# Cross-attention and FP4 feed-forward on one core: the softmax's turn moved from TensorE to transposing DMAs, in slots of four heads

## The reference, cut to what matters

```python
x = x + xattn(layernorm(x), ctx)       # q from x, k and v from ctx
    logits = einsum('bhqk,bhnk->bhqn', q, k) / 8
    attn   = softmax(logits)           # over the 154 context rows
    heads  = einsum('bhqn,bhnv->bhqv', attn, v);  out = hid @ w_out.T
x = x + ffn(layernorm(x))              # 704 wide
    fp4_linear(x, w): x and w are each rounded to FP4 in blocks of 16, then einsum
    out = fp4_linear(silu(gate) * up, w_down)
```

## Time and profile before

| | |
|---|---|
| runs | 435.9, 433.01 and 435.87 us, median 435.87 |
| profiled execution | span 431.8 us from the first to the last instruction; no time of its own stands beside it |
| PE, DVE, ACT, POOL busy | 367.8, 348.9, 276.8, 200.1 us |
| mean granted clock of TensorE | 0.968 |

### The profile page before, as it was taken

How to read it: one execution, slowest core, us unless ns; L and a number is a source line. 1 busy time by engine, 2 the same in 40 slices (tenths; PEclk the granted TensorE clock), 3 DMA queues, 4 the chain that set the end, 5 groups by cost and what they waited for, 6 DMA issues and landing times.

```text
span 431.8 us, 9502 instructions
## 1 busy us (share of the span) xinstructions
PE 367.8 (85%) x3691; PEld 282.7 (65%) x3691; DVE 348.9 (81%) x676; ACT 276.8 (64%) x869; POOL 200.1 (46%) x235
## 2 busy tenths in 40 slices
PE   1864798999989989999899967988785999999985
PEld 1543664777868778778687755855563776777764
DVE  2989866996988969879889798569779799999692
ACT  4766979887997897879978775365142255433331
POOL 3455313354454543544545544026643657676710
PEclk9998699999999999999999997999899799999999
DMA  7970000000000000000000000000000000000001
GB/s 218 322 275 1 2 2 0 5 2 0 4 2 2 0 4 2 1 2 4 2 2 2 2 1 2 0 2 2 1 2 13 14 20 18 14 24 14 24 27 36
DMA packets 8445, 11.48 MB, mean 27 GB/s; under 512 B 524, under 2 KB 6352, under 8 KB 8401
## 3 DMA queue, kind: packets, MB, share of 16 engines
q1 hardware_dynamic: 8401, 10.88, 8.0%
HBM read 8.78 MB, written 2.10 MB: 25 GB/s over the span
## 4 chain that ended last, share of the span: by engine, by line
DVE 38%; ACT 28%; PE 28%; issue 3%; DMA 1%; POOL 0%; SPq 0%; DVEq 0%; ACTq 0%
ACT arena L747 14%; PE ps L398 7%; PE ps L400 7%; PE ps L399 7%; ACT arena L738 5%; ACT pT L756 4%; DVE arena L1058 4%; DVE negmax L998 4%; DVE arena L1056 3%; DVE arena L989 3%; DVE arena L1182 2%; DVE pT L1007 2%; PE ps L544 2%; DVE blk_h L1023 2%; DVE arena L1148 2%
## 5 line engine op out<-in xcount | busy, mean ns | idle before, releaser
L747 ACT ACTIVATE arena<-ps,negmax 128x154 f32<-128x154 f32 x256 | 98.4, 430 | 16.1 <-DVE negmax L998 16.0
L1238 POOL TENSOR_TENSOR arena<-arena,rinv 128x104 f32<-128x104 f32 x64 | 23.1, 361 | 114.9 <-DVE rinv L1003 114.9
L1239 POOL TENSOR_TENSOR arena<-arena,rinv 128x512 f32<-128x512 f32 x64 | 66.7, 1042 | 0.0
L1007 DVE TENSOR_TENSOR pT<-ps,pT 128x512 f16<-128x512 f32 x80 | 54.6, 682 | 13.0 <-ACT pT L756 13.0
L747 ACT ACTIVATION_READ_ACCUMULATOR arena<-ps,negmax 128x1 f32 x256 | 63.4, 248 | 0.0
L544 PE MATMUL ps<-ident,arena 128*128 128x128 f32 x320 | 53.7, 292 | 4.0 <-DVE pT L1007 4.0
L756 ACT ACTIVATE pT<-ps 128x512 f16<-128x512 f32 x80 | 51.5, 644 | 5.5 <-PE ps L544 5.4
L998 DVE TENSOR_REDUCE negmax<-ps 128x4 f32<-128x616 f32 x64 | 50.2, 785 | 0.3 <-PE ps L534 0.2
L534 PE MATMUL ps<-kT_h,arena 64*128 64x154 f16 x512 | 37.8, 233 | 12.7 <-ACT arena L747 12.0
L398 PE MATMUL ps<-arena,xnT_h 128*128 128x352 f16 x128 | 40.8, 319 | 8.5 <-DVE xnT_l L1066 6.7
L544 PEld LDWEIGHTS ps<-ident,arena 128*128 128x128 f32 x320 | 35.2, 145 | 14.9 <-issue 7.9
(11 more groups left out here) (153 smaller groups left out, 1039.3 us busy)
## 6 DMA issues: line engine op xcount, KB each, us to landing
out_dram<-arena SPq DMA_DIRECT2D x16, 128.0 KB, 1.7
xs<-in_x_dram SPq DMA_DIRECT2D x2, 512.0 KB, 7.3
arena<-in_L_xattn_w_out_dram SPq DMA_DIRECT2D x1, 1024.0 KB, 11.9
xs<-in_x_dram SPq DMA_DIRECT2D x2, 384.0 KB, 6.7
wffn<-in_L_ffn_w_down_dram SPq DMA_DIRECT2D x1, 704.0 KB, 9.3
wffn<-in_L_ffn_w_gate_dram SPq DMA_DIRECT2D x1, 640.0 KB, 7.7
wffn<-in_L_ffn_w_up_dram SPq DMA_DIRECT2D x1, 640.0 KB, 8.3
arena<-in_ctx_dram SPq DMA_DIRECT2D x1, 308.0 KB
```

What stands on the lines that cost most here:

```text
L747: last = act.activation(prob[:, s, h * L:(h + 1) * L], ps[:, 2 * (j % 2) + k % 2, (k // 2) * L:(k // 2 + 1) * L], ACT.Exp, bias=negmax[:, ...
L1007: dve.tensor_tensor(quad_T(1, i, s, g), ps[:, T_BANK + (s + g) % 2, :].rearrange("p (c n) -> p c n", c=4), quad_T(0, i, s, g), ALU.subtrac ...
L1239: pool.tensor_tensor(v[:, :, 0:P], v[:, :, 0:P], r.to_broadcast([P, 4, P]), ALU.mult).then_inc(normed, 1)
```

## The change

The probabilities are no longer turned on TensorE. GpSimd normalises into a buffer of its own (`normal`, four quads of 640 fp32 columns: 4 x 128 and 4 x 32 for the last rows). VectorE casts all 640 columns to fp16 (`high_p`), GpSimd subtracts for the low half (`low_p`), and SP issues one transposing DMA for each quad, 128 rows by 1,280 fp16 columns (320 KB), from `split` to `pT`. The turned halves have one semaphore for each of the four quads of a tile (`turned[j]`), and there are four places in `split`, so a cast waits for the transposing DMA of four quads earlier.

The loop is over slots, one quad each, eight to a step, in every engine's stream (`slot(n)`). The other products are tasks at given slots: `tasks_of`. They share one list, one set of semaphores (`task_mm`, `task_high`, `task_low`) and the three banks 4, 5 and 7; bank 6 is the projection's. VectorE's half of a task comes one slot after ScalarE's. The projection is cut in eight parts, one in each slot. The six transposes of the FFN's gate and up weights go into slots 57 to 62, and all four `heads` of the last step into the FFN's first two tiles. Some buffers of the FFN lie elsewhere.

```diff
+SLOTS = 2 * STEPS * QUADS
+CHUNK = 5 * P
+        def rows_at(i):
+            return 8 * (i - 1) + (3 if i == 1 else 2)
+        def query_at(i, j):
+            return 8 * (i - 1) + ((5, 6, 7, 8) if i == 1 else (4, 6, 8, 9))[j]
+        def heads_at(i, j):
+            return 8 * (i + 1) + (2, 3, 5, 7)[j]
+        def wt_at(n):
+            return (57, 57, 60, 60, 62, 62)[n]
+        def high_by_act(n):
+            return False
+        def low_by_dve(n):
+            return False
...
 # SP
+            def turn_p(n):
+                i, s, j = place(n)
+                wait_low(sp, n)
+                if i == 1: sp.wait_ge(task_mm, TASK_AT[VALUES[-1]] + 1)
+                if i >= 2: sp.wait_ge(task_mm, TASK_AT[("h", i - 2, j)] + 1)
+                sp.dma_start_transpose(pT[:, i % 2, j, :, :, s * P:(s + 1) * P].rearrange("p a c n -> p (a c) n"),
+                                       split[:, j]).then_inc(turned[j], 16)
...
 # TensorE
-            def turn_p(i, s, g):
...
-                    last = pe.transpose(ps[:, T_BANK + (s + g) % 2, k * P:(k + 1) * P], v, ident[:, :])
+            for n in range(SLOTS):
+                score(n)
+                if parts_of(n): project(*parts_of(n))
+                for t in tasks_of(n):
+                    task(t)
...
 # ScalarE
-            def p_high(i, s, g):
...
+            def slot(n):
+                if n >= 2 and high_by_act(n - 2): high_p(n - 2)
+                exps(n)
+                for t in tasks_of(n):
+                    high(t)
...
 # VectorE
-            def p_low(i, s, g):
...
+            def high_p(n):
+                j = n % QUADS
+                dve.wait_ge(normed, n + 1)
+                wait(dve, turned[j], 16 * (n // QUADS))
+                dve.tensor_copy(part_of(j, 0), normal[:, j]).then_inc(high_dve, 1)
+            def slot(n):
+                row_max(n)
+                if n >= 1: inverse(n - 1)
+                if n >= 2 and not high_by_act(n - 2): high_p(n - 2)
+                if n >= 1:
+                    for t in tasks_of(n - 1):
+                        low(t)
+                if n >= 2 and low_by_dve(n - 2): low_p(n - 2)
+                if i == 0: first(n)
+                if m == 3 and i >= 2: add_attention(i - 2)
...
+                    if m == 5: minus_grid_w(w, 0)
+                    if m == 6: minus_grid_w(w, 1)
...
+                if 52 <= n < 57: layernorm(0, EARLY, 2 * LN_STEPS, [n - 52])
...
 # GpSimd
+            def low_p(n):
+                j = n % QUADS
+                wait_high(pool, n)
+                pool.tensor_tensor(part_of(j, 1), normal[:, j], part_of(j, 0), ALU.subtract).then_inc(low_pool, 1)
+            def slot(n):
+                if n >= 1: norm(n - 1)
+                if n >= 2 and not low_by_dve(n - 2): low_p(n - 2)
...
```

More of the change, by code:

```diff
@@ L274, in ht_bank, with wait_high, wait_low @@
+        def wait_high(eng, n):
+            before = [m for m in range(n + 1) if high_by_act(m) == high_by_act(n)]
+            eng.wait_ge(high_act if high_by_act(n) else high_dve, len(before))
+        def wait_low(eng, n):
+            before = [m for m in range(n + 1) if low_by_dve(m) == low_by_dve(n)]
+            eng.wait_ge(low_dve if low_by_dve(n) else low_pool, len(before))
         def ht_bank(i, s):
@@ L428, in _, with next_task @@
                 last.then_inc(job_mm, 1)
-            def next_o(job):
-                wait(pe, o_done, O_AT[job])
-                return ps[:, O_BANK, :]
+            def next_task(t):
+                n = TASK_AT[t]
+                before = [m for m in range(n) if task_bank(m) == task_bank(n)]
+                if before: pe.wait_ge(task_low, before[-1] + 1)
+                return task_out(t)
             def turn_o(n):
@@ L599, in _ @@
             pe.wait_ge(job_low, J_END)
-            for j in range(QUADS):
-                score(0, 0, j)
-            steps(pe, attention)
+            for n in range(SLOTS):
+                score(n)
+                if parts_of(n): project(*parts_of(n))
+                for t in tasks_of(n):
+                    task(t)
             def turn_xq(i, s):
@@ L607, in turn_xq @@
                 wait(pe, xqt_low, t)
+                if t == 0: pe.wait_ge(task_low, max(n for n in range(BODY) if task_bank(n) == XT_BANK) + 1)
                 for c in range(KC):
@@ new lines, in weights_high @@
+            def weights_high(n):
+                kind, c, j0 = WT_JOBS[n]
+                o = task_out(("w", n))
+                if kind == "w1":
+                    w = min(4, W1T - j0) * P
+                    last = act.activation(w1_h[:, c, j0 * P:j0 * P + w], o[:, 0:w], ACT.Copy, scale=-FS)
+                else:
+                    act.wait_ge(pad2_zero, 1)
+                    for k in range(2):
+                        m = min(P, F - (j0 + k) * P)
+                        last = act.activation(wdT[0:m, j0 + k, 0:D], o[0:m, k * D:(k + 1) * D], ACT.Copy, scale=-FS)
+                last.then_inc(task_high, 1)
@@ L745, in exps, with high @@
+            def high(t):
+                act.wait_ge(task_mm, TASK_AT[t] + 1)
+                if t[0] == "x": x_high(t[1])
+                elif t[0] == "q": q_high(t[1], t[2])
+                elif t[0] == "w": weights_high(t[1])
+                else: o_high(t)
+            high(("x", 0))
+            def exps(n):
+                i, s, j = place(n)
+                act.wait_ge(max_done, n + 1)
+                wait(act, normed, n - 3)
                 for k in range(4):
                     h = 4 * j + k
-                    last = act.activation(prob[:, s, h * L:(h + 1) * L],
+                    last = act.activation(prob[:, j, k * L:(k + 1) * L],
@@ L831, in _ @@
+            act.wait_ge(w_scaled, 1)
+            split_part("v", wv_h, 1.0, 0)
+            high(("q", 0, 0))
+            split_part("v", wv_h, 1.0, 1)
+            for j in range(1, QUADS):
+                high(("q", 0, j))
             act.activation(unused[:, 0:1], biasT[:, 0:1], ACT.Exp)
-            for j in range(QUADS):
-                exps(0, 0, j)
             act.wait_ge(pad_zero, 3)
-            steps(act, attention)
+            for n in range(SLOTS):
+                slot(n)
+            if high_by_act(SLOTS - 2): high_p(SLOTS - 2)
@@ L1106, in stats_of @@
+            low(("x", 0))
             def stats_of(i):
@@ L1279, in _ @@
+            for n in range(SLOTS):
+                slot(n)
+            norm(SLOTS - 1)
+            for n in (SLOTS - 2, SLOTS - 1):
+                if not low_by_dve(n): low_p(n)
             round_x(0)
```

650 lines of the change are left out of this document (300 added, 350 removed).

## The result

The changed kernel takes 444.07 us (median of 4, 443.27 to 444.89) against 434.88 for the kernel before on the same chip: a ratio of 1.0228, 95% interval 1.0188 to 1.0268. It is slower, by 1.9 to 2.7%, where 420 was forecast as faster. The profiled execution has a span of 442.6 us, against 415.8 in the forecast's sum: 26.8 us are missing. That execution took 444.45 us, 1.9 over its own span. The forecast had added 4.1 for this, the difference between the median of the executions and the span of one whose own time it did not have, so against the measured median it is 24.1 us off.

A forecast was written before the change was run, and what follows sets the result against it. TensorE was taken as fullest before, GpSimd after, at 27.9 us a step. Terms of -7.5, -1, -12, +3 and +1.5 us, together -16, gave a span of 415.8; with 4.1 over the span, 420 us, range 406 to 436.

The forecast's parts named there:

- (b): The 48 quads after the first 12: 3.5 us each, 168 us in all, -1 us (-11 to +11).
- the layer norm: Normalisation of steps 0 to 4 on VectorE, slots 52 to 56: 19 small held instructions beside a full GpSimd, +3 us.
- R1: Rival, chance 0.15: GpSimd holds VectorE's cast and three rounding instructions a step; at 0.9 us mean hold, 442 us.
- the forecast's own signs: Middle steps: GpSimd busy over 90% and steps of 28 us if right; wrong if under 26 or over 30 us.
- The sign that did tell: Middle steps: GpSimd's waits for reciprocals, 12.6 us a step before the change, would be gone.
- R4: Rival, chance 0.03: TensorE, waiting in every slot, drops to 1.2 GHz; half of each step there gives about 440 us.
- (a): First 12 quads: shorter casts and fewer waits on VectorE bring 48.6 us to 41, -7.5 (-11 to -2).
- (c): From the last four quads to the first gate-and-up: three intervals 10.2 us, then 10.5; 20.7 in all, -12 (-13 to -8).
- (d): The FFN's first tiles: one more `heads` each and four parts of the projection, +1.5 us.
- R2: Rival, chance 0.12: the transposing DMAs bound the kernel, from 3.5 us each; at 5.3 us each, 545 us.
- The upper end: Highest estimate for a quad's transposing DMA: 1,280 packets at 66 ns each, 5.3 us a slot.
- R3: Rival, chance 0.12: the cast is not held and costs GpSimd nothing or less than taken; 3.2 us a slot, 402 us.

The follow-up runs named there:

- run 1: Changed kernel with the 64 casts on ScalarE instead of VectorE: 420.37 us, ratio 0.9666 to the kernel before.
- run 7: Changed kernel without the nine Newton-step instructions in the layer norm of steps 0 to 4: 442.5 us, ratio 1.0183 to the kernel before.
- runs 10 and 11: Changed kernel with four PSUM banks for tasks of slots 0 to 9, then also the later ring begun at the bank longest free: 440.95 and 442.55 us.
- Runs 8 and 9: Changed kernel with the seventh projection's second half behind the first gate-and-up, then also block scales ahead of the attention sum: 448.81 and 444.48 us.
- run 6: Changed kernel with the 64 transposing DMAs replaced by plain DMAs of the same bytes: 444.87 us, ratio 1.0234 to the kernel before.

## Why the prediction was wrong

**The step that failed** is (b), "48 quads at 3.5 us", by its premise that the fullest engine is always fed. Its terms for GpSimd held: 25.5 us without casts on VectorE were forecast and 25.62 measured, 27.9 with them forecast and 27.7 measured (the mean over the slots 12 to 48). A step there took 29.5 us, so GpSimd stood idle for 1.8 of it, where the forecast had nothing; these make 1.5 us over the forecast's 28.0, and in 4.5 steps the missing 6.7. Over all 48 quads it was 187.0 us against 168 and the 3 of the layer norm, so 16.0 of the 26.8 us; the other 9.3 of these are the layer norm's slots, and 8.9 more are the first 12 slots, both below.

The argument against R1, "the cast follows the reciprocal at once, and GpSimd's next instruction starts only when that has ended", is where the idle time hid. It holds for the casts at which GpSimd has run dry and waits for the reciprocal: they take 0.46 us, and it is GpSimd's 0.36 us that become 0.52 (136.93 in the step above). It fails once GpSimd is behind: the low half of the quad before is then ready, needs neither this reciprocal nor this cast, and is running when the cast begins. So it was for 32 of the 64 casts. A held cast makes VectorE late, and a late VectorE lets GpSimd run dry a few slots on. The mean hold was 923 - 460 = 0.46 us over all casts, and about 0.54 over the 11 instructions of the step shown, under the 0.64 from which R1 was to decide. R1 was priced as if VectorE had to become full; it was enough that VectorE came late. That its 442 us lie near the 444 measured is luck.

Two of the forecast's own signs were too weak to tell: GpSimd was busy for 94% of those steps, as it had asked, and 29.5 us is not over 30. The sign that did tell is that its waits for reciprocals stayed (2.2 us in the step shown, 44.9 over the whole run).

**R4**, given 0.03, took part: 6.8 us of a step at the lower level where the forecast's likeliest case had none. In the step shown, TensorE's slow stretch stands before 0.87 of GpSimd's 2.2 idle us, and the 1.31 came without it. The low clock goes when VectorE is on time (run 1: 1.00 granted in a step). How much it adds by itself, beside the wait that it follows, stays open.

**The layer norm** was a mis-sized term: 19 instructions, called "small held instructions beside a full GpSimd", at 3 us, which is 0.16 us each, the price of free ones, though the earlier trace rows had one at 1.13 us. They kept VectorE busy for 11.4 us in the slots 52 to 56 (ten at 0.17 or 0.18, nine held, up to 1.38), while VectorE had no room:

```profile
238.00:254.00 16.00, 11.31 (x117) 8.26 (x115) 15.73 (x29) 7.45 (x33) 12.09 (x12) 0.89 0.47 82
```

By busy time that is 8.4 of the 9.3 us missing in the slots 48 to 60; how much a cure of it would return is less (run 7: 5.3 us at slot 57, 2.5 at slot 60), so the rest of the 9.3 is not accounted for.

**(a), the first 12 slots**, took 49.9 us, not 41. The forecast worked from VectorE's busy time, but no engine is over 75% busy there. TensorE waits for VectorE's halves of tasks, in part through the banks (runs 10 and 11), and 5.7 us once for ScalarE's normalised rows. Removing the casts brought 2.8 of the 8.9 us (run 1), though the first nine casts are not held (0.46 us each). The banks brought 1.6 to 2.0, but the kernel with plain DMAs also had 1.9 less, for which I have no cause. The fewer waits of which the forecast made 7.5 us did not come, and why stays open.

**(c) and (d)** were wrong apart and right together: 27.7 and 145.6 us against 20.7 and 152.4, so 173.3 against 173.1. In (c) the three intervals took 8.9 us against 10.2, and from the last row maxima to the gate-and-up it was 18.8 against 10.5; 4.7 of that is the seventh projection's second half, for which (c) has no term. Runs 8 and 9 show that such work only changes sides of the line. That the two errors cancel to 0.2 us is in part luck: the FFN came out 5.3 us shorter than before where 1.5 more were forecast, and no run prices that. Held casts of 1.6 us in the last slots took part too.

**R2** fell: the 64 transposing DMAs land after 3.4 us, against 3 taken, no wait on one is in the trace, and plain DMAs change nothing (run 6). It fell by more than the 3.5 us from which it was to decide suggest, since a DMA is issued before the one ahead has landed (128.46 against 128.88 for two of them). By the packets' own times in the trace, a DMA's first packet comes 1.2 us after its issue and its packets run for 1.7 us (medians). The upper end had the number of packets right and their time wrong: a DMA has 1,280 of 256 bytes and 32 of 4, but they take 23 ns each, not 66.

The Trainium skill's figure on the page VectorE: DVE Perf Modes (section on the three transpose paths), 1,309 ns a block, times ten blocks in a row, would have been an estimated 13 us; ten blocks landed in 3.4, so they don't run in a row here. The 261 GB/s on the Trainium skill's page DMA: Bandwidth & Descriptors (Latency and other measured facts) gave an estimate of 1.3 us for the bytes alone; the packets here took 1.7, and 3.4 with what stands before and behind them.

**R3** fell with the held casts.

## What to carry to other kernels

An instruction that an engine's neighbour can hold costs more than its hold: price the queue behind it, up to the engine that is the bound. Ask what the neighbour has ready to run at the moment when the held instruction comes: if it is behind, it has something. When a full engine feeds on a chain through others, the sum of its work is a lower end, not a forecast; here the fullest engine stood idle for 1.8 us of every 29.5. Give small instructions of the held kind the price of the held one. And where two stretches share an engine that works through, forecast their sum.

## What the runs showed of the hardware

- The hold goes by the form of VectorE's instruction, not by its length or its data: with source and target in SBUF, a copy (0.46 us free), a tensor-tensor (0.79 free) and a scalar-tensor-tensor (0.69 at the shortest) were held up to 1.9 or 2.0 us; a reduction over the same 640 elements stayed at 0.78 to 0.82. A reduction over groups of one element is thus a cast that GpSimd did not hold in any of 64.
- A held copy of 640 elements ended 0.35 us after the GpSimd instruction beside it, in 35 of 36 held ones (0.59 in the other).
- The same forms hold GpSimd: its 104-column product took 0.36 us on average beside the reduction, 0.53 beside the copy and 0.81 beside the tensor-tensor.
- Ten elements a partition are enough: 0.17 us free, up to 1.38 beside a GpSimd instruction.
- A transposing DMA of 128 x 1,280 fp16 lands 3.4 us after its issue, a plain one of the same bytes after 3.2. The transposing ones show the DMA engines busier: 34.6% of 16 engines' span on that queue, against 25.8%. Both move packets of 256 bytes.
